# First layer's weights and its product with x made in the first gather stage; the convolution adds it

## What is computed

```python
h = _bn(x @ w1.T + b1, g1, beta1)
agg = jax.ops.segment_sum(h[src], dst, num_segments=n)
conv = agg @ wr.T + br + h @ wroot.T
h = jax.nn.gelu(conv, approximate=False)
out = _bn(h @ w2.T + b2, g2, beta2) + x
```

## Time and profile before

| | |
|---|---|
| median of three runs | 7227.28 us |
| the profiled execution | 7232.81 us, its span 7230.7 us |
| PE busy | 4566.8 us (63%), 16502 matmul instructions |
| POOL busy | 5129.1 us (71%) |
| DVE, ACT busy | 2692.8 us (37%), 831.0 us (11%) |
| mean granted clock of TensorE | 0.799 |

### The profile page before, as it was taken

How to read it: one execution, slowest core, us unless ns; L and a number is a source line. 1 busy time by engine, 2 the same in 40 slices (tenths; PEclk the granted TensorE clock), 3 DMA queues, 4 the chain that set the end, 5 groups by cost and what they waited for, 6 DMA issues and landing times.

```text
span 7230.7 us, 61411 instructions
## 1 busy us (share of the span) xinstructions
PE 4566.8 (63%) x16502; PEld 3365.8 (47%) x16502; DVE 2692.8 (37%) x5977; ACT 831.0 (11%) x1870; POOL 5129.1 (71%) x4804
## 2 busy tenths in 40 slices
PE   5666669866667665555557555557555554555657
PEld 3455449655545554344446444435444443343436
DVE  7543112755555554321113211114111124444445
ACT  0000003322232222100000000000000000000002
POOL 7777750288888885577775777775777776777774
PEclk9888779988888887777778777778877776767678
DMA  3333343266666666433333333334333336666661
GB/s 90 108 116 116 105 129 103 30 72 71 72 71 71 72 71 140 130 105 105 105 105 117 104 105 105 105 105 123 105 105 105 105 105 191 191 195 193 196 193 51
DMA packets 495386, 810.82 MB, mean 112 GB/s; under 512 B 95106, under 2 KB 365332, under 8 KB 495060
## 3 DMA queue, kind: packets, MB, share of 16 engines
q0 software_dynamic: 300288, 615.29, 37.5%
q1 hardware_dynamic: 194772, 191.57, 8.2%
HBM read 652.63 MB, written 153.86 MB: 112 GB/s over the span
## 4 chain that ended last, share of the span: by engine, by line
POOL 60%; issue 22%; PE 9%; DVE 5%; DMA 3%; SPq 0%; DVEq 0%; ACT 0%; POOLq 0%; ACTq 0%
POOL ring L499 47%; POOL sums_by_src L521 12%; PE acc L560 2%; PE acc L652 2%; PE high L565 2%; DMA ring<-table_x,idx_dst 1%; DMA sums_by_src<-ring,E 1%; PE acc L565 1%; DVE onehot L1208 1%; DVE H L1091 1%; PE high L560 1%; DVE ring L1218 1%; DVE X L1239 0%; PE high L551 0%; PE acc L551 0%
## 5 line engine op out<-in xcount | busy, mean ns | idle before, releaser
L652 PE MATMUL acc<-ring,onehot 128*128 x8320 | 2904.2, 511 | 2023.2 <-DVE onehot L1208 2009.1
L652 PEld LDWEIGHTS acc<-ring,onehot 128*128 128x128 f32 x8320 | 2013.9, 253 | 2886.6 <-issue 2527.3
L499 POOL DMA_INDIRECT ring<-table_g,idx_dst x2346 | 2236.4, 953 | 894.0 <-issue 713.7
L1208 DVE TENSOR_TENSOR onehot<-iota_row,dl_dst 128x512 f32<-128x512 f32 x1040 | 719.3, 692 | 2952.3 <-SPq L284 2557.0
L521 POOL DMA_INDIRECT sums_by_src<-ring,E x782 | 1208.1, 1545 | 584.3 <-ACT high L1002 345.3
L499 POOL DMA_INDIRECT ring<-table_x,idx_dst x782 | 828.5, 1059 | 269.6 <-issue 259.5
L499 POOL DMA_INDIRECT ring<-in_x_dram,idx_dst x782 | 780.5, 998 | 256.8 <-issue 251.7
L816 PE MATMUL high<-H,ring 128*128 x1664 | 553.9, 491 | 445.1 <-ACT high L1002 433.4
L816 PEld LDWEIGHTS high<-H,ring 128*128 128x128 f32 x1664 | 379.8, 239 | 542.3 <-issue 480.0
L1451 DVE TENSOR_SCALAR ring<-acc,E 128x128 f32<-128x128 f32 x832 | 283.8, 402 | 575.7 <-PE acc L569 575.7
L1218 DVE TENSOR_TENSOR ring<-ring,E 128x1024 f32<-128x1024 f32 x196 | 240.0, 1225 | 546.0 <-DMA ring<-table_x,idx_dst 546.0
(11 more groups left out here) (266 smaller groups left out, 2858.6 us busy)
## 6 DMA issues: line engine op xcount, KB each, us to landing
E<-in_edge_attr_dram SPq DMA_DIRECT2D x781, 128.0 KB, 2.9
ring<-table_g,idx_dst POOLq DMA_INDIRECT x2346, 2.7
ring<-sums_by_src SPq DMA_DIRECT2D x36, 512.0 KB, 4.7
table_g<-H SPq DMA_DIRECT2D x36, 512.0 KB, 5.4
sums_by_src<-ring SPq DMA_DIRECT2D x2, 6272.0 KB, 38.4
ring<-in_x_dram,idx_dst POOLq DMA_INDIRECT x782, 2.8
sums_by_src<-ring,E POOLq DMA_INDIRECT x782, 3.8
ring<-table_x,idx_dst POOLq DMA_INDIRECT x782, 3.4
```

The costliest lines, as they stand in the source:

```text
L499: pool.indirect_dma_start(out=ring_v[:, b % SLOTS, 0:D], out_offset=None, in_=table[name][:, :], in_offset=bass.IndirectOffsetOnAxis(ap=id ...
L652: pe.matmul(acc4[:, ds(to, width)], onehot[:, (q * BATCH + j) % ONEHOTS, :], ring[:, ds(slot, width)], start=False, stop=True, skip_group_ ...
L1208: last = tt(onehot[:, s:s + BATCH, :], iota_row[:, :].unsqueeze(1).to_broadcast((P, BATCH, P)), dl_ap[which][:, q * BATCH:(q + 1) * BATCH] ...
```

## The change

The four weights are loaded at the start, turned in quads 32 and 33 and copied by DVE in quad 34; three of them stay in a part of H that is free by then. After the last tile of the statistics pass (quad 136) the rows of edges are turned in quad 138 (160 before). In quads 140 to 146 DVE sums the statistics, takes the inverse root by itself (an integer first guess and four Newton steps on two columns) and, with PE, makes the folded weights. SP loads all tiles of x into H in groups 139 to 151. In quads 154 to 192 the tiles, two at a time (a duo, 25 of them in three quads for two duos), are turned, copied in place, multiplied with wt_b and moved back into H with the constant added (`x_part`). The loads of XR stay. The convolution loop multiplies A's tile alone, DVE adds the sum to H's tile, ACT applies Gelu to a whole tile in one operation, and the product with w2 comes three tiles behind the turn (two before).

```diff
...
-        y_rows_in = [bias[:, i, :] for i in range(3)] + [wt[w_][:, i, :] for w_ in "bd" for i in range(DH)]
+        y_rows_in = [bias[:, i, :] for i in range(3)] + [wt["b"][:, i, :] for i in range(DH)]
...
+        ROWS_AT = Y0 + YS * (T - 1) + 2
+        W_AT = ROWS_AT + 2
+        X_AT = W_AT + 14
...
+        def x_duos(q):
+            return [d for d in range(ND) if X_AT + d + d // 2 == q]
...
+                    if n == 0:
+                        x_rows(k)
+
+            def x_rows(k):
+                if k == ROWS_AT + 1:
+                    sp.wait_ge(sm("y_turned"), T)
+                    sp.wait_ge(sm("rows_known"), 2)
+                at = 4 * (k - ROWS_AT - 1)
+                for t in range(at, min(T, at + 4)) if at >= 0 else ():
+                    if t == 34:
+                        sp.wait_ge(sm("conv_weights"), 1)
+                    rows_ = min(P, N - t * P)
+                    load(tile(H, t)[0:rows_, :], a["x"][t * P:t * P + rows_, :], sm(f"x_in{t // XG}"))
...
-            load(wt["d"][:, :, :], a["L0_gnn_w1"].rearrange("(h o) k -> o h k", o=P), sm("wnat_in"))
+            for k, name in zip("abcd", ("w2", "wr", "wroot", "w1")):
+                weight_rows(k, "L0_gnn_" + name)
...
-            for q, name in enumerate(("L0_gnn_w1", "L0_gnn_wr", "L0_gnn_wroot", "L0_gnn_w2")):
-                load(wnat[:, q, :, :], a[name].rearrange("(h o) k -> o h k", o=P), sm("wnat_in"))
...
+            def first_weights(q):
+                if q == Y0 - 8:
+                    pe.wait_ge(sm("tables_late"), 2)
+                    pe.wait_ge(sm("wnat_in"), 64)
+                    turn_weight(bank[4], "d")
+                    turn_weight(bank[5], "b")
+                if q == Y0 - 7:
+                    turn_weight(bank[6], "c")
+                    turn_weight(bank[7], "a").then_inc(sm("w_turned"), 1)
+                if q == W_AT + 2:
+                    pe.wait_ge(sm("bn1"), 1)
+                    for h in range(DH):
+                        one(bank[6][:, 0:D], chunk(bias[:, 1, :], h), wr_v[:, h, :], h == 0, h == DH - 1)
+                    for o in range(DH):
+                        for h in range(DH):
+                            last = one(bank[7][:, o:o + 1], wroot_v[:, h, o * P:(o + 1) * P], bn_s[:, 3, h:h + 1],
+                                       h == 0, h == DH - 1)
+                    last.then_inc(sm("conv_mm"), 1)
+                if q == W_AT + 4:
+                    pe.wait_ge(sm("bn1"), 2)
+                    weight_product(bank[4], wr_v)
+                if q == W_AT + 5:
+                    weight_product(bank[5], wroot_v).then_inc(sm("conv_mm"), 1)
+
+            def x_part(q):
+                for d in x_duos(q):
+                    if d == 0:
+                        pe.wait_ge(sm("conv_weights"), 1)
+                    for t in duo(d):
+                        if t % XG == 0:
+                            pe.wait_ge(*x_landed(t, 1))
+                    if d >= 2:
+                        pe.wait_ge(sm("y_xT"), T + d - 1)
+                    for t in duo(d):
+                        last = turn(bank[4 + d % 2][:, t % 2 * D:(t % 2 + 1) * D], tile(H, t))
+                    last.then_inc(sm("y_turned"), 1)
+                for d in x_duos(q - 1):
+                    pe.wait_ge(sm("y_xT"), T + d + 1)
+                    if d >= 2:
+                        pe.wait_ge(sm("x_part"), d - 1)
+                    for t in duo(d):
+                        last = to_features(bank[6 + d % 2][:, t % 2 * D:(t % 2 + 1) * D], [(wt["b"], tile(H, t))])
+                    last.then_inc(sm("y_mm"), 1)
...
-            for i in range(T + 2):
+            for i in range(T + 3):
                 if i < T:
                     if i >= 2:
                         pe.wait_ge(sm("conv_aT"), i - 1)
-                        pe.wait_ge(sm("conv_xT"), i - 1)
-                    if i % XG == 0:
-                        pe.wait_ge(sm(f"x_in{i // XG}"), 16 * len(range(i // XG, T, 3)) + 16 * min(XG, T - i))
                     turn(bank[i % 2], tile(X, i)).then_inc(sm("conv_turned"), 1)
-                    turn(bank[i % 2][:, D:2 * D], tile(XR, i)).then_inc(sm("conv_turned"), 1)
                 if 1 <= i <= T:
                     t = i - 1
-                    pe.wait_ge(sm("conv_weights"), 1)
                     pe.wait_ge(sm("conv_aT"), t + 1)
-                    pe.wait_ge(sm("conv_xT"), t + 1)
                     pe.wait_ge(sm("conv_dg"), t + 1)
                     if t >= 2:
-                        pe.wait_ge(sm("conv_gelu"), t - 1)
-                    to_features(bank[2 + t % 2], [(wt["a"], aT0[t % 2]), (wt["b"], tile(H, t))],
+                        pe.wait_ge(sm("conv_sum"), t - 1)
+                    to_features(bank[2 + t % 2], [(wt["a"], aT0[t % 2])],
                                 [(bias[:, 0, :], dg[t % 2])]).then_inc(sm("conv_mid"), 1)
-                if i >= 2:
-                    t = i - 2
+                if i >= 3:
+                    t = i - 3
                     pe.wait_ge(sm("conv_gelu"), t + 1)
                     if t >= 2:
                         pe.wait_ge(sm("y_stats"), T + t - 1)
...
-            for q in range(4):
-                act.wait_ge(sm("w_turned"), q + 2)
-                sc.copy(wt["abcd"[q]][:, :, :].rearrange("p h d -> p (h d)"), bank[4 + q]).then_inc(sm("w_copied"), 1)
-            root(bn_s[:, 1, :], bn_s[:, 0, :], 1)
-
-            for i in range(T + 1):
+            for i in range(T + 2):
                 if i < T:
-                    act.wait_ge(sm("conv_turned"), 2 * i + 2)
+                    act.wait_ge(sm("conv_turned"), i + 1)
                     if i >= 2:
                         act.wait_ge(sm("conv_mid"), i - 1)
                     sc.copy(aT0[i % 2], bank[i % 2][:, 0:D]).then_inc(sm("conv_aT"), 1)
-                    sc.copy(tile(H, i), bank[i % 2][:, D:2 * D]).then_inc(sm("conv_xT"), 1)
-                if i >= 1:
-                    t = i - 1
-                    act.wait_ge(sm("conv_mid"), t + 1)
-                    for h in range(DH):
-                        last = sc.activation(chunk(tile(H, t), h), chunk(bank[2 + t % 2], h), ACT.Gelu, bias=bn_s[:, 4, h:h + 1])
-                    last.then_inc(sm("conv_gelu"), 1)
-            root(bn_s[:, 1, :], bn_s[:, 0, :], 2)
+                if i >= 2:
+                    t = i - 2
+                    act.wait_ge(sm("conv_sum"), t + 1)
+                    sc.activation(tile(H, t), tile(H, t), ACT.Gelu).then_inc(sm("conv_gelu"), 1)
+            root(bn_s[:, 1, :], bn_s[:, 0, :], 1)
...
+            def inverse_root(out_, v, half, bits):
+
+                link(ts(bits, v.bitcast(I32), 1, None, ALU.logical_shift_right))
+                link(copy(half, bits))
+                link(ts(out_.bitcast(I32), half, -1.0, float(0x5f3759df), ALU.mult, ALU.add))
+                for _ in range(4):
+                    link(tt(half, out_, out_, ALU.mult))
+                    link(tt(half, half, v, ALU.mult))
+                    link(ts(half, half, -0.5, 1.5, ALU.mult, ALU.add))
+                    link(tt(out_, out_, half, ALU.mult))
+
+            def first_weights(q):
+                if q == Y0 - 6:
+                    dve.wait_ge(sm("w_turned"), 1)
+                    copy(wt["a"][:, :, :].rearrange("p h d -> p (h d)"), bank[4])
+                    for i, k in enumerate(turned_w):
+                        last = copy(turned_w[k], bank[5 + i])
+                    link(last)
+                    dve.sem_inc(sm("w_copied"), 1)
+                if q == W_AT:
+                    dve.wait_ge(sm("y_stats"), T)
+                    for h in range(DH):
+                        last = nc.vector.bn_aggr(bn_mv[:, h, :], stats[:, h, :])
+                    link(last)
+                    link(ts(bn_s[:, 0, :], bn_mv[:, :, 1], EPS, None, ALU.add))
+                if q == W_AT + 1:
+                    inverse_root(bn_s[:, 1, :], bn_s[:, 0, :], bn_s[:, 2, :], cols_i[:, :])
+                    dve.wait_ge(sm("cols_in"), 16 * 7)
+                    norm_columns(bn_mv[:, :, 0], pcol[:, 1, :], pcol[:, 2, :], pcol[:, 0, :])
+                    for h in range(DH):
+                        last = ts(chunk(bias[:, 1, :], h), ones[:, :], bn_s[:, 3, h:h + 1], None, ALU.mult)
+                    link(last)
+                    dve.sem_inc(sm("bn1"), 1)
+                if q == W_AT + 3:
+                    dve.wait_ge(sm("conv_mm"), 1)
+                    link(copy(bias[:, 0, :], bank[6][:, 0:D]))
+                    link(tt(bn_s[:, 4, :], bank[7][:, 0:DH], pcol[:, 3, :], ALU.add))
+                    for wk in (wr_v, wroot_v):
+                        for h in range(DH):
+                            last = ts(wk[:, h, :], wk[:, h, :], bn_s[:, 2, h:h + 1], None, ALU.mult)
+                    link(last)
+                    dve.sem_inc(sm("bn1"), 1)
+                if q == W_AT + 6:
+                    dve.wait_ge(sm("conv_mm"), 2)
```

(84 more changed lines are left out.)

90 lines of the change are left out of this document (27 added, 63 removed).

## The result

The changed kernel takes 7147.37 us (median of five runs, 7145.54 to 7154.49), the kernel before 7229.84 (five runs, 7226.42 to 7230.96): a ratio of 0.9889, 95% interval 0.9878 to 0.99. The forecast was 7149.3. The profiled execution takes 7147.14 us (span 7145.1), 85.7 less than that of before.

What follows compares the result with a forecast made beforehand. POOL, issuing indirect DMAs, was 60% of the chain; PE alone paced the convolution loop. -27.8 - 54.2 + 2 + 2 = -78.0 us from 7232.8 leaves 7154.8, less 5.5 to the median: 7149.3 us, range 7142 to 7172.

Steps and rivals of the forecast that it cites:

- The chain before the loop: Between last gather pairs and first convolution product: weight steps move into the gather, first product at 1049.0 us, gain 27.8 us.
- The loop: Convolution loop over 49 tiles: PE alone paces it, 1560 to 1074 matmul instructions, 119.9 us long, gain 54.2 us.
- The clock at the loop's start: First 6 us or so of the convolution loop may run at 1.2 GHz: 0 to 3 us lost, 2 taken.
- POOL in the gather: First gather stage: new DVE steps from SBUF to SBUF slow POOL, bounds 0 and 10 us, 2 taken; PSUM copies cost nothing.
- the 1041 that I had named as a sign: End of the first gather stage: the last gather comes at about 1041 us, as before.
- PE in the gather: Quads 154 to 192: PE nearly full at 4.5 of 4.66 us a quad, last 16 quads give back 34 us; cost 0.
- the full clock that I had supposed: Gather quads with the product with x: PE, being nearly full, should run at the full clock (1.00 in the loop).
- slowed as in the heavy part: Rival, gather quads 140 to 192: POOL starts 38 gathers in 50 us instead of 41, 19 us lost, 7166 us; chance 0.11.
- the loop isn't held by its path: Rival denied here: convolution loop stays at 3.6 us a tile through product, add, gelu, second product; 7204 us, chance 0.06.
- the last third isn't PE's: Rival denied here: PE stays at the lower clock in the gather's last third, 7.4 us a quad, 7243 us; chance 0.04.
- the end moved with the loop: Answers the rival that something else holds the next stage, so the end does not move: 7227 us, chance 0.02.
- the bound of 3.2 us by the cited section: First gather stage: by the Trainium skill's page alone, new scalings, copy and fills cost POOL up to 3.2 us, small steps nothing.

Runs made afterwards that it cites:

- e2: Changed kernel without the product of bias and degree in the convolution loop (18 instead of 22 matmul instructions a tile, part of the result left out); 7129.11 us.
- e5: Changed kernel with gelu again in two operations of half a tile; 7143.99 us, ratio 0.9883 to the kernel before.
- e3: Changed kernel with each product with x in the gather made twice; 7158.59 us, ratio 0.9892 to the kernel before.
- e4: Changed kernel with each product with x in the gather made three times; 7162.86 us, ratio 0.9903 to the kernel before.
- e7: Changed kernel with ACT instead of SP issuing the third loads of x; 7155.98 us, ratio 0.989 to the kernel before.
- e8: Changed kernel with four more DVE additions of 128x512 behind each duo's move in the gather, both inputs in SBUF; 7165.93 us, ratio 0.9902.
- e9: Changed kernel with four more DVE additions of 128x512 behind each duo's move, one input in PSUM and one in SBUF; 7162.76 us, ratio 0.9898.
- e1: Changed kernel with only the weights made early: product with x stays in the loop, no third load of x, gelu in halves; 7213.85 us, ratio 0.998.

## Why the prediction was right

- **The chain before the loop: -27.8 forecast, -28.0 measured** (28.92 to 0.89 us between last pairs and first product). The diagonal ends last, as the prediction has it, 0.12 us behind ACT's copy of tile 0.
- **The loop: -54.2 forecast, -54.1 measured** (174.58 to 120.47), by 1074 instructions as counted; e2 shows that PE's count holds it, and e5 that gelu does not. In seven kernels with these instructions (after, e3, e4, e5, e7, e8, e9) the loop takes 120.47 or 120.48 us.
- **The clock at the loop's start: +2 forecast, 0 measured.** e1 shows the price (2 us after 11.5 us of idle time), after a condition that wasn't met. It was closer than the 0 looks: in after the last pairs still ran at 0.50 (1.2 GHz) up to 1050.2, and the clock was back at 1.00 only 2.1 us before the loop. In all seven kernels above, though, the loop's length shows no loss.
- **POOL in the gather: +2 forecast, +3.1 in its gathers (780.5 to 783.6), 3.5 at the last pairs' end.** The size was near by luck; the reason was wrong. I charged the new steps from SBUF to SBUF, and e1, which has them all, shows 0.2 us in the gathers for them. The last gather came at 1044.4 us and not at the 1041 that I had named as a sign. The long gathers stand elsewhere, two of them here (after):

```profile
742.33 0.69 DVE L1250 TENSOR_TENSOR onehot<-iota_row,dl_dst 128x512 f32<-128x512 f32 x1 [0.79 <-DVE bias L1399]
...
742.66 1.18 POOL L527 DMA_INDIRECT ring<-in_x_dram,idx_dst  x1 [0.30 <-issue]
...
833.92 0.69 DVE L1250 TENSOR_TENSOR onehot<-iota_row,dl_dst 128x512 f32<-128x512 f32 x1 [3.56 <-issue]
834.00 1.43 POOL L527 DMA_INDIRECT ring<-in_x_dram,idx_dst  x1 [0.30 <-issue]
```

  All 16 between 700 and 980 us start inside a one-hot, an old operation with both inputs in SBUF; 29 gathers of 800 to 990 us that start inside the new copies and moves from PSUM keep 0.95. The count of one-hots is the same (59 before, 60 after, in these 280 us), but 18 gathers start inside one instead of 4: they have moved against each other. By e1 it isn't the weights' steps; whether the loads of x, the product with x or chance does it stays open (e7), as kernels with the same gather stage differ by 2.4 us.
- **PE in the gather: 0 forecast, 0 measured**, with more room than I gave it. Starts are hidden behind the product with x (e4). The clock there is 0.93, not the full clock that I had supposed.
- **The rivals.** POOL starts 40 or 41 gathers in 50 us, so it isn't slowed as in the heavy part; the loop isn't held by its path (e2, e5); the last third isn't PE's (0.93, and e3 and e4 with two and three times the work); the end moved with the loop.
- **The rest.** Stage by stage the profiled pair gives 79.8 us against 78.0 forecast; the last gather stage's 6 us were in no step, and the medians, 82.5 apart, hold some of such spread. The sum gives -78.6 at the end of the loop (-28.0 - 54.1 + 3.5) against -78.0. That 7149.3 lies within 2 us of the median is partly luck: three runs of before gave 7227.28 to start from, five gave 7229.84.
- **Slips of the working that change nothing.** The trace has one new fill in the gather (L1364) and not three, and six copies of weights from PSUM and not five. The gather of 1.22 us in the earlier trace rows is held by one tensor_tensor and not by two (below). In the bound of 3.2 us by the cited section the fills don't belong, as they have no input: 2.4.

## What to carry to other kernels

Before work is moved under a stage that another engine paces, count the room in the pacing engine's periods and the stretch that follows without such work: it gives back what fell behind, at the difference of the two periods. A loop with one engine busy without a pause is priced by its instructions alone (e2), and steps on other engines are free while they hide behind it (e5); how much work must lie between them, no run here shows. Beside indirect DMAs, take one input of a two-input operation from PSUM where there is a choice.

## What the runs showed of the hardware

- A gather that starts while a DVE operation with two SBUF inputs runs is held, and ends 0.82 us after that one: 742.33 + 0.69 + 0.82 = 743.84 = 742.66 + 1.18; 833.92 + 0.69 + 0.82 = 835.43 = 834.00 + 1.43; so too the one of before. In the twelve traces, from 200 to 1050 us, 945 gathers start more than 0.05 us behind the start of such an operation (of over 0.4 us) and more than 0.13 (0.95 - 0.82) ahead of its end, and all 945 end so, within 0.02 us. One that is under way is not held: e8's of 863.66 keeps 0.95 us though a one-hot starts at 864.04; nor, mostly, one that starts together with the operation (e8's of 866.16; 48 of 57 that start in its first 0.05 us).
- At a chance phase one operation of 0.69 us would cost (0.69 - 0.13)^2 / 2 / 1.25 = 0.125 us of POOL, an estimate from these lengths: 12 us for e8's 96. Measured are 57 x (1.079 - 0.948) = 7.5 in the gathers that start inside one, and 7.2 between e8's and e9's sums. So the starts are not spread evenly over the operation.
- The Trainium skill ("SBUF — State Buffer", Who interferes with whom) says that a DVE instruction with two SBUF inputs contends with a GpSimd one that reads SBUF, and that one with at most one SBUF input, outside the two-port modes, leaves it alone: e8 (1.079 us) and e9 (0.948) agree, if a gather counts as an instruction that reads SBUF. Its inference, weighed in the prediction, that tensor_tensor does not hold up descriptor generation, does not fit e8, where the instructions that issue the gathers are held; which part of such an instruction waits, the traces don't show.
- Behind the loop, the rows z are made at a mean granted clock that is back at 1.00 after 25 us in after, and after 75 us in e9 (0.80, 0.86, 0.93, 1.00 in steps of 25 us from 1175), with the same instructions. From the loop's statistics to POOL's next start it is 134.5 us in after, 141.0 in e9, and 138.95 in e5, whose clock lies between (0.93 from 1200 to 1250). These 6 us are why a step of the gather is read at the end of the loop and not from the time of a run.
